# Order of scores, turns and value products in the 64-wide attention layers, and who empties the projections' banks

## The reference, cut to what matters

```python
q = layer_norm(x) @ Wq                  # 256 x 1024, 16 heads of 64
k, v = split(context @ Wkv, 2)          # 256 x 1024 each
p = softmax(q_h @ k_h.T * scale + mask) # 256 x 256 for each of 16 heads
out = concat_h(p @ v_h) @ Wo            # 256 x 128
x = x + out (+ bo, or layer_norm(out) * g_out in layer 3)
```

## Time and profile before

| | before |
|---|---|
| median of 3 runs | 1899.88 us |
| the profiled execution | 1894.79 us |
| its span | 1893.1 us |
| TensorE matmul busy | 1579.8 us (83%) |
| VectorE busy | 1160.7 us (61%) |
| ScalarE busy | 880.3 us (47%) |
| GpSimd busy | 289.3 us (15%) |
| chain that ended last | TensorE 50%, VectorE 21%, issue 12%, ScalarE 11% |

### The profile page before, as it was taken

One profiled execution on the slowest core, in us unless ns is written; L12 is line 12 of the kernel. 1 busy time (PEld: TensorE's weight loads), 2 busy tenths in 40 slices (PEclk: granted clock), 3 DMA queues, 4 the chain that ended last, 5 costly groups with the idle time before them and its releaser, 6 DMA issues.

```text
span 1893.1 us, 38137 instructions
## 1 busy us (share of the span) xinstructions
PE 1579.8 (83%) x13117; PEld 1153.5 (61%) x13117; DVE 1160.7 (61%) x2971; ACT 880.3 (47%) x1893; POOL 289.3 (15%) x441
## 2 busy tenths in 40 slices
PE   4889999989999779997466277999968888899887
PEld 3567776766666568886244154666645666666665
DVE  4766666675666668887311255554545767777781
ACT  1555555563333557776144043333314545555552
POOL 2000000011011224331211523000010011111111
PEclk9999999999999889998579589999978989999999
DMA  9100000000000300000011020000000000000000
GB/s 261 54 2 0 0 0 0 0 1 1 1 0 0 92 1 0 0 0 2 14 46 36 15 53 1 1 1 0 0 0 1 1 1 0 0 0 0 0 2 23
DMA packets 32087, 28.85 MB, mean 15 GB/s; under 512 B 6058, under 2 KB 26419, under 8 KB 31812
## 3 DMA queue, kind: packets, MB, share of 16 engines
q1 hardware_dynamic: 30980, 25.66, 4.7%
q0 software_dynamic: 1024, 2.10, 0.4%
HBM read 21.52 MB, written 6.23 MB: 15 GB/s over the span
## 4 chain that ended last, share of the span: by engine, by line
PE 50%; DVE 21%; issue 12%; ACT 11%; POOL 3%; DMA 1%; SPq 1%; ACTq 0%; DVEq 0%; POOLq 0%
PE bank L1360 43%; PE bank L1364 7%; DVE PTs L2110 4%; ACT Pm L1208 4%; DVE negm L2093 2%; DVE negm L2090 2%; DVE VxF L700 2%; DVE Qz L2380 2%; ACT VxF L1167 1%; ACT Pm L1321 1%; ACT PTs L1166 1%; DVE st L1902 1%; ACT Pm L1285 1%; POOL yn L940 1%; POOL token_rows_by_expert L1086 1%
## 5 line engine op out<-in xcount | busy, mean ns | idle before, releaser
L1208 ACT ACTIVATE Pm<-bank,negm 128x256 f32<-128x256 f32 x784 | 320.6, 472 | 323.6 <-DVE negm L2093 198.1
L2110 DVE TENSOR_TENSOR PTs<-bank,PTs 128x512 f16<-128x512 f32 x384 | 252.3, 683 | 85.3 <-ACT PTs L1166 84.8
L1360 PE MATMUL bank<-kT,Qz 64*128 64x256 f32 (+2 forms) x1568 | 297.5, 403 | 3.7 <-issue 1.3
L1364 PE MATMUL bank<-ident,Pm 128*128 128x128 f32 x1568 | 230.7, 280 | 37.1 <-DVE PTs L2110 17.3
L1360 PE MATMUL bank<-xHL,R 128*128 (+3 forms) x1008 | 235.4, 381 | 13.9 <-DVE Qz L2380 13.8
L1364 PEld LDWEIGHTS bank<-ident,Pm 128*128 128x128 f32 x1568 | 182.5, 143 | 103.3 <-ACT Pm L1208 50.2
L1166 ACT ACTIVATE PTs<-bank 128x512 f16<-128x512 f32 (+1 forms) x388 | 219.6, 604 | 52.3 <-PE bank L1364 41.8
L1360 PEld LDWEIGHTS bank<-kT,Qz 64*128 64x128 f32 (+1 forms) x1568 | 183.2, 189 | 74.8 <-issue 59.0
L1321 ACT ACTIVATE Pm<-bank,upback 128x512 f32<-128x512 f32 x168 | 115.3, 686 | 199.7 <-PE bank L1360 199.4
L2093 DVE TENSOR_REDUCE negm<-bank 128x2 f32<-128x512 f32 x264 | 176.2, 686 | 41.8 <-PE bank L1360 39.2
L1360 PE MATMUL bank<-VxF,PTs 128*128 128x65 f16 (+3 forms) x4672 | 186.6, 187 | 16.2 <-DVE PTs L2110 15.4
(11 more groups left out here) (266 smaller groups left out, 1883.5 us busy)
## 6 DMA issues: line engine op xcount, KB each, us to landing
token_rows_by_expert<-wpad SPq DMA_DIRECT2D x10, 256.0 KB, 4.0
R<-in_L_ffn_ew SPq DMA_DIRECT2D x2, 1024.0 KB, 7.0
R<-in_L_ffn_w SPq DMA_DIRECT2D x1, 2048.0 KB, 9.8
R<-in_L_xattn_Wkv SPq DMA_DIRECT2D x2, 768.0 KB, 6.5
Qz<-token_rows_by_expert SPq DMA_DIRECT2D x23, 64.0 KB, 1.9
expert_rows<-Qz SPq DMA_DIRECT2D x23, 64.0 KB, 1.5
R<-in_L_ffn_w SPq DMA_DIRECT2D x1, 1408.0 KB, 12.9
R<-in_L_xattn_Wq SPq DMA_DIRECT2D x2, 512.0 KB, 3.7
```

The costliest lines, as they stand in the source:

```text
L1208: last = act.activation(Pm[:, k % 4, qt * S:(qt + 1) * S], bank[k % 2][:, qt * S:(qt + 1) * S], ACT.Exp, bias=negm[:, k % 4, qt:qt + 1])
L1360: return pe.matmul(o, l, r, start=start, stop=stop)
L1364: return pe.transpose(o, i, ident[0:n, 0:n])
L2110: dve.tensor_tensor(PTl[:, k % 4, :], bank[2 + k % 2][:, :], PTh[:, k % 4, :], ALU.subtract).then_inc(s.pt[1].sem, 1)
```

## The change

In slot p the scores of pair p now come first, then the turns of pair p-1, fills_a, the rounding of pair p-1 on ScalarE (a new step `high`, which was part of `turn`), av and norm of pair p-2, `low` of pair p-1 on VectorE, and fills_b. The epilogue gets two slots in place of one. The tables are new, with at most three fills to a slot. In these two layers a fill's bank is now emptied by kind: q, k, outT, outN, sn and turns by ScalarE, ln and snt by VectorE, every v half and half (high by ScalarE, low by VectorE). The semaphore that counts the reads of a bank stays with the bank (`bank_read`), whichever engine reads. The one new wait is VectorE's for dn before it writes nsn.

```diff
-WIDE = {0: ([], [("v", 1), ("q", 3)]), 1: ([("outT", -1)], [("k", 3)]),
-        2: ([("woa", 0)], [("wo", 0), ("resid", 0)]), 3: ([("outT", 0)], [("v", 3)]),
-        4: ([("q", 0)], [("ln", 0), ("k", 0)]), 5: ([("q", 1), ("outT", 1)], [("v", 0)]),
-        6: ([("k", 1)], [("v", 2)]), 7: ([("outT", 2), ("q", 2)], [("k", 2)])}
-WIDE_NULL = {0: ([], [("v", 1), ("k", 3)]), 1: ([("outT", -1), ("outN", 0)], [("q", 3), ("turns", 0)]),
-             2: ([("woa", 0)], [("wo", 0), ("resid", 0)]), 3: ([("outT", 0)], [("v", 3)]),
-             4: ([("q", 0)], [("k", 0), ("resid2", 0)]), 5: ([("outT", 1)], [("v", 0), ("q", 1)]),
-             6: ([("k", 1), ("q", 2)], [("v", 2), ("sn", 0)]), 7: ([("outT", 2), ("ln", 0)], [("snt", 0), ("k", 2)])}
+WIDE = {0: ([("outT", -2)], [("k", 3)]), 1: ([("q", 3)], [("v", 1)]),
+        2: ([("outT", -1)], [("v", 3)]), 3: ([("woa", 0)], [("wo", 0), ("resid", 0)]),
+        4: ([("outT", 0)], [("q", 0)]), 5: ([("k", 0)], [("v", 0), ("ln", 0)]),
+        6: ([("outT", 1), ("q", 1)], [("k", 1)]), 7: ([("q", 2)], [("v", 2), ("k", 2)])}
+WIDE_NULL = {0: ([("outT", -2)], [("k", 3)]), 1: ([("q", 3)], [("v", 1)]),
+             2: ([("outT", -1), ("outN", 0)], [("v", 3)]), 3: ([("woa", 0)], [("wo", 0), ("resid", 0)]),
+             4: ([("outT", 0)], [("q", 0), ("turns", 0)]), 5: ([("k", 0)], [("v", 0), ("resid2", 0)]),
+             6: ([("outT", 1), ("q", 1)], [("k", 1), ("sn", 0)]), 7: ([("q", 2), ("ln", 0)], [("v", 2), ("snt", 0), ("k", 2)])}
...
-    st = [("turn", a - 2), ("turn", b - 2), ("low", a - 2), ("low", b - 2)]
-    if p < 8:
-        st += [("pair", a), ("softmax", a), ("softmax", b), ("null", p)]
+    st = [("pair", a), ("softmax", a), ("softmax", b), ("null", p)] if p < 8 else []
+    if p < 9:
+        st += [("turn", a - 2), ("turn", b - 2)]
     st += fills_a
-    st += [("av", a - 2), ("av", b - 2), ("norm", p - 1)]
+    if p < 9:
+        st += [("high", a - 2), ("high", b - 2)]
+    st += [("av", a - 4), ("av", b - 4), ("norm", p - 2)]
+    if p < 9:
+        st += [("low", a - 2), ("low", b - 2)]
     return st + fills_b
...
+def on_act(A, kind, m):
+    return kind in ("q", "k", "outT", "outN", "sn", "turns") if A.dh == 64 else m % 2 == 0
...
-                        elif kind == "turn" and (A.n != 2 or k % 2 == 0):
+                        elif kind == ("high" if A.dh == 64 else "turn") and (A.n != 2 or k % 2 == 0):
...
-                        elif kind in FILLS and m % 2 == 0:
+                        elif kind in FILLS and on_act(A, kind, m):
                             need(act, s.ring.filled, b * BATCH_FILLS.get(A.n, 0) + (m + 1))
-                            att_evac(A, move, kind, k, b, kinds, bank_of(m)).then_inc(s.ring.act.sem, 1)
+                            att_evac(A, move, kind, k, b, kinds, bank_of(m)).then_inc(bank_read(s, m).sem, 1)
```

More of the change, by code:

```diff
@@ L174, in att_schedule @@
             fills_a, fills_b = [[step for step in part if kept(step)] for part in (WIDE_NULL if A.null else WIDE)[p]]
[L175 to L179, removed]
+            st += [(kind, k) for kind, k in pair_steps(p, fills_a, fills_b)
+                   if k >= 0 or not first or kind not in ("turn", "high", "av", "norm", "low")]
             if last and A.n == 0 and 1 <= p:
@@ L200, in att_prologue @@
         return [("q", j) for j in range(4)] + [("turns", 0)]
-    return [("q", 0), ("q", 1), ("q", 2)] + ([("sn", 0), ("snt", 0), ("turns", 0)] if A.null else [])
+    return [("q", 0), ("q", 1), ("q", 2)] + ([("sn", 0), ("snt", 0)] if A.null else [])
 def att_epilogue(A):
     if A.dh == 64:
-        st = [(kind, k - 16 if kind != "norm" else k - 8) for kind, k in pair_steps(8, [], [])]
-        return st + [("outT", -1), ("outN" if A.null else "turns", 0), ("woa", 0), ("wo", 0), ("resid", 0)] + (
+        st = []
+        for p in (8, 9):
+            st += [(kind, k - (8 if kind == "norm" else 16)) for kind, k in pair_steps(p, [], [])]
+            st.append(("outT", p - 10))
+        return st + [("outN" if A.null else "turns", 0), ("woa", 0), ("wo", 0), ("resid", 0)] + (
             [("resid2", 0)] if A.null else [])
@@ L554, in att_counts @@
             fills = sum(s[0] in FILLS for k in kinds for s in kind_steps(A, k))
-            vfills = [m % 2 for k in kinds if A.n != 2 for kind, j, m, _ in steps(A, 0, k) if kind == "v"]
+            vfills = [m % 2 or A.dh == 64 for k in kinds if A.n != 2 for kind, j, m, _ in steps(A, 0, k) if kind == "v"]
             return dict(vhigh=sum(vfills), vlow=len(vfills) - sum(vfills), filled=fills, act=(fills + 1) // 2, dve=fills // 2, scores=nh, negmax=nh, exp=nh, dn=8 * B if A.null else 0,
@@ L619, in steps @@
             for kind, k in st:
-                if kind in ("wo", "snt"):
+                if kind == "snt" or kind == "wo" and A.dh != 64:
                     assert n % 2 == 1, (A.n, kinds, n)
@@ L625, in v_of @@
         def v_of(A, kinds, parity):
-            return [m for kind, k, m, _ in steps(A, 0, kinds) if kind == "v" and m % 2 == parity]
+            return [m for kind, k, m, _ in steps(A, 0, kinds) if kind == "v" and (m % 2 or A.dh == 64) == parity]
         def v_count(A, parity):
@@ L1240, in body @@
                                  bank[2 + k % 2][:, :]).then_inc(s.pt[0].sem, 1)
-                        elif kind == "v" and A.n != 2 and m % 2:
+                        elif kind == "v" and A.n != 2 and (m % 2 or A.dh == 64):
                             need(act, s.ring.filled, b * BATCH_FILLS[A.n] + (m + 1))
@@ L1507, in fill @@
                         ms = [m_ for kind_, _, m_, _ in steps(A, b, kinds) if kind_ == "sn"][0]
-                        need(pe, s.ring.dve if ms % 2 else s.ring.act, b * (per // 2) + ms // 2 + 1)
+                        if ms % 2 != m % 2:
+                            need(pe, bank_read(s, ms), b * (per // 2) + ms // 2 + 1)
                         plain(pe)
@@ L2119, in body @@
                                                          ALU.mult, ALU.subtract).then_inc(up_low, 1)
[L2120 removed]
+                        elif kind == "v" and A.n != 2 and (m % 2 or A.dh == 64):
                             need(dve, s.vhigh, b * v_count(A, 1) + v_done(A, b, kinds, m, 1))
[L2122 removed]
+                            v_low(A, dve, k, bank_of(m)).then_inc(bank_read(s, m).sem, 1)
                         elif kind == "v" and A.n != 2:
@@ L2174, in body @@
                             if A.null:
-                                dve.tensor_copy(osb[:, :, :], ps).then_inc(s.ring.dve.sem, 1)
-                                need(dve, s.ring.dve, b * (BATCH_FILLS[A.n] // 2) + mw // 2 + 1)
+                                dve.tensor_copy(osb[:, :, :], ps).then_inc(bank_read(s, mw).sem, 1)
+                                need(dve, bank_read(s, mw), b * (BATCH_FILLS[A.n] // 2) + mw // 2 + 1)
                                 stats(osb, 2, chain, s.ostats.sem, mvo)
@@ L2197, in body @@
                             dve.tensor_copy(x[:, bass.ds(bl * 2, 2), :], xnew[:, 0:2, :])
-                        elif kind in FILLS and m % 2 and kind != "wo":
+                        elif kind in FILLS and not on_act(A, kind, m) and kind != "wo":
                             need(dve, s.ring.filled, b * BATCH_FILLS.get(A.n, 0) + (m + 1))
-                            att_evac(A, move, kind, k, b, kinds, bank_of(m)).then_inc(s.ring.dve.sem, 1)
+                            if kind == "snt" and kinds != "prologue":
+                                need(dve, s.dn, b * 8 + 8)
+                            att_evac(A, move, kind, k, b, kinds, bank_of(m)).then_inc(bank_read(s, m).sem, 1)
                     used[kinds] = n[0]
```

8 lines of the change are left out of this document (4 added, 4 removed).

## The result

The changed kernel takes 1884.4 us (four runs, 1881.7 to 1886.8), beside 1899.8 us (1899.2 to 1900.2) for the kernel before on the same chip: ratio 0.992, 95% interval 0.990 to 0.994. It is faster by 0.8%, which is 25 us less gain than the forecast and 2.4 us above the upper end of the range. The profiled execution took 1881.7 us; its span is 1879.9 us.

A forecast was written before the change was run, and what follows sets the result against it. TensorE was taken as the bound, its waits as the loss. Layer 0's -28.4 and layer 3's -12.3 sum to -40.7 us: 1899.9 - 40.7 = 1859.2 us (profiled execution 1854.1); forecast's own range 1848 to 1870, whole range 1842 to 1882.

The forecast's parts named there:

- the 1.6 us wait: Layer 0's steady batch: TensorE waits 1.6 us for banks 6 and 7, for ScalarE's Qz; claimed to go.
- the batch at clock 0.96: Another layer 0 batch, 48.2 us with one 1.6 us wait; its 1.7 us taken as gone, bounds 0 and 1.7.
- the 0.4 us for k1: Layer 0, slot 6: k1, the third fill, waits for outT1, emptied by ScalarE behind late exponentials; 0.4 us lost per batch.
- the floor of 43.0 us: Layer 0's steady batch: TensorE's work without gaps, summed from distances between starts in one slot; 43.0 us.
- GpSimd's pause: Loop's first pass: GpSimd's 6.88 us late start after ctxb would be covered in the new order; 6.3 and 7.0 us go.
- rival A: Pause after loop entry belongs to program layout and falls behind resid; gives back up to 6.3 + 7.0: 1872.5; chance 0.14.
- Layer 3's steady batch: TensorE's floor 44.5 plus bank waits and lateness 6.3 gives 50.8 us, only 0.4 less than 51.2.
- the 6.7 us that it called gaps: Layer 3's steady batch before the change: 6.7 us per batch taken as gaps over TensorE's floor of 44.5 us.
- the waits before k1 and for VxF in layer 3: Signs of a right forecast: TensorE waits 2 us or more before k1 and over 1 us for VxF L700.
- B: Layer 3's four big bank waits each 0.6 us longer, 17 us in all: 1876; sign: steady batch over 52; chance 0.14.
- C: Closed chain over ScalarE and VectorE bounds every slot, so slower; at 1.0 us more a slot +36, 1936; chance 0.07.
- D: Layer 3's lateness is half of that walked, 3 us x 7 = 21: 1838; chance 0.13.

The follow-up runs named there:

- resid2 early: The changed kernel with layer 3's resid2 moved from the end of fills_b to fills_a of slot 5; 1872.8 us, ratio 0.987.
- the two-fill slots: Kernel with resid2 early, sn in slot 1, k2 ahead of v2; layer 3's v3, q0, k0, q1 moved: 1850.6 us; with rounding before fills_a too: 1863.2 us.

## Why the prediction was wrong

The profiled execution is 27.6 us over the forecast of 1854.1. From the starts of the batches in both traces:

| stretch | forecast, us | measured, us |
|---|---|---|
| ahead of layer 0's attention | 0 | -0.7 |
| layer 0: first, second, then five steady | -2.1, -9.4, -17.2 | -2.5, -7.4, -17.8 |
| layer 0: last, and epilogue | +0.3 | +2.1 |
| stages between | 0 | +2.7 |
| layer 3: first, second | -3.2, -7.4 | -2.7, -3.4 |
| layer 3: five steady | -2.0 | +14.1 |
| layer 3: last, and epilogue | +0.3 | +2.5 |
| sum | -40.7 | -13.1 |

**Layer 0.** The gain came as forecast: 43.3 us measured, 43.4 forecast, the 1.6 us wait and the batch at clock 0.96 both gone. That the number is met to 0.1 us is in part luck: the 0.4 us for k1 did not appear, and the floor of 43.0 us was 0.3 us low.

**GpSimd's pause** is the smaller failed step. I counted it from ctxb, because in the earlier trace rows ctxb was the later of its two inputs: the statistics were complete at 110.66 us (mv in VectorE's rows, 110.41 + 0.25), ctxb at 114.16, and the start was at 121.04. In the new order ctxb was copied by 104.59 and the statistics are the later; the pause came after them:

```profile
112.75 0.25 DVE L1921 BATCH_NORM_AGGREGATE mv<-st 128x2 f32<-128x6 f32 x2
120.22 0.18 POOL L949 TENSOR_SCALAR ve<-mv 128x2 f32<-128x2 f32 x1 [15.62 <-issue]
123.19 0.41 PE L1377 MATMUL bank<-ident,yn 128*128 128x128 f32 x2 [2.21 <-POOL yn L953]
```

113.0 + 7.2 us to the start, and ln 2.2 us late instead of covered by 5. That is the mechanism of rival A, the pause falling behind resid, at 2.2 us of the 6.3 that A allowed in this layer. In layer 3 the pause was covered, apart from 0.6 us more before k1 (2.79 in place of 2.17 us): 54.7 us against 54.4 in a steady batch. In the next pass the same instruction starts 0.5 us after its statistics (1537.63 + 0.25 to 1538.41 us). The Trainium skill (Runtime: NRT & Kernel Launch, Instruction fetch mechanics) lays an instruction-fetch stall to a taken branch whose target is outside what is held. No run here shows that this is such a stall: the pause is in the first pass of the loop alone, and it begins only when the later input is there. Its cause was not tested.

**Layer 3's steady batch** is the step that failed: its sum is TensorE's floor plus waits, with nothing for the low clock that follows waits. It accounts for 16 of the 27.6 us (the clock lacks 15.5 us there) and, in the second batch, for most of 4 more (3.4 us). Its waits were right (6.3 walked, 5.7 measured), the lateness that makes them too: the maxima of slot 6 start 2.0 us after the scores, 2.1 forecast, and OT's bank is free at 5.3, 5.4 forecast. The floor was 0.8 us low (51.05 - 5.7 = 45.3 where I had 44.5). The missing term is the clock, 3.3 us a batch (54.4 - 51.05). The prediction named the low clock itself where it explained the second batches, and then left it out of the steady ones. A wait of 1.58 us in a batch at clock 1.00 made this look safe. It was also not the only wait of the old batch; the longest was another, for a bank that VectorE empties:

```profile
PE bank L1360 <- DVE OT L1892: 1.8, 1, 1.8
...
PE bank L1364 <- DVE OT L1892: 1.2, 1, 1.2
```

With the 1.6 us of the earlier trace rows and 0.3 us more that makes 4.9 us in four waits, where the prediction named one, and the 6.7 us that it called gaps were 4.9 us of waits over a floor that it had too low. No steady batch of the kernel before had a fall in spite of them. So 4.9 us with the longest of 1.8 kept the clock and 5.7 us with the longest of 2.17 did not, but no run shows where the line is: with resid2 early a batch waits about 4.3 us, the longest 1.4 to 1.6, and had a fall in five batches of five.

Of the signs that the prediction named, the gone wait for Qz in layer 0 and the waits before k1 and for VxF in layer 3 came as written; a steady batch over 52 us, its sign for B, came for another reason.

**The rivals.** B foretold the direction, a batch of 53 us or more, but by longer waits, and they are not longer. C did not decide in the steady batches of the changed kernel; the two-fill slots show how near it is. D is ruled out: the walked lateness is there in full.

**Stages between.** Nothing in them was changed, and they gave back 2.7 us. The first batch of layer 1 had one wait of 1.9 us at clock 1.00 before (29.5 us) and has one of 2.4 us at clock 0.95 now (31.1 us); a stretch of layer 1's routed part has clock 0.54 in place of 0.59 (38.4 us in place of 37.3). Both go with a lower clock; what made that wait longer was not looked for. The last batch of layer 0, at clock 0.92 where the earlier trace rows have 0.96, and layer 3's last (waits of 2.0 us for Pm) take 2 us each more than walked, inside the bounds given. Whether the old order in these batches would give that back was not tested.
